# A recurrence and its output stage in one block: half-batches first, POOL and ACT written out

## What is computed

```python
x = x + ttt_linear(layer_norm(group_norm(x)))      # tokens in order, 64 chunks of 16
x = x + relu(W @ [g, descriptor(g)] + bias)         # g = group_norm(x)
```

## Time and profile before

| | us |
|---|---|
| median of 3 runs | 687.34 (686.9 to 690.31) |
| profiled execution | 686.33 |
| its span, first to last instruction | 684.4 |
| PE busy | 523.5 (76%) |
| DVE busy | 492.6 (72%) |
| ACT busy | 332.1 (49%) |
| POOL busy | 376.9 (55%) |

### The profile page before, as it was taken

The page is one execution under the profiler, slowest core; times in us unless marked ns, Lnnn a source line. Parts: engine busy times, 40 slices in busy tenths (PEclk is TensorE's granted clock), DMA queues, the critical chain, the costliest instruction groups (busy, mean ns, idle before and its releaser), DMA issues. The chain is left out here.

```text
span 684.4 us, 30685 instructions
## 1 busy us (share of the span) xinstructions
PE 523.5 (76%) x12150; PEld 364.9 (53%) x12150; DVE 492.6 (72%) x1548; ACT 332.1 (49%) x1044; POOL 376.9 (55%) x659
## 2 busy tenths in 40 slices
PE   0399999996488777777777777777777399859997
PEld 0143344434377666666666666666666155435552
DVE  6356767665678989899999989898998357528331
ACT  0434442225255555555555555555555577544432
POOL 0368888775356555566665556655565647321323
PEclk9999999997555555555555555555555699979999
DMA  9101111114800000000000000000000700000113
GB/s 346 45 12 39 41 31 32 31 31 95 185 4 1 0 0 0 0 0 0 0 0 0 0 0 0 0 0 0 0 2 4 273 5 0 1 1 1 62 69 117
DMA packets 9850, 24.55 MB, mean 36 GB/s; under 512 B 1845, under 2 KB 2510, under 8 KB 9550
## 3 DMA queue, kind: packets, MB, share of 16 engines
q1 hardware_dynamic: 9806, 24.01, 11.4%
HBM read 11.42 MB, written 4.19 MB: 23 GB/s over the span
## 5 line engine op out<-in xcount | busy, mean ns | idle before, releaser
L762 PE MATMUL PS<-work 32*32 32x32 f32 x4064 | 85.5, 238 | 73.1 <-DVE work L911 65.4
L762 PEld LDWEIGHTS PS<-work 32*32 32x32 f32 x4064 | 81.2, 152 | 83.5 <-issue 79.5
L963 POOL TENSOR_TENSOR work<-work,mask 128x256 f32<-128x256 f32 x64 | 46.7, 730 | 83.4 <-DVE work L911 71.8
L751 PE MATMUL PS<-work 64*32 64x64 f32 x2048 | 69.5, 308 | 19.9 <-ACT work L1006 16.9
L500 PE MATMUL PS<-X,work 128*128 (+3 forms) x160 | 72.1, 597 | 6.7 <-ACT X L640 6.4
L751 PEld LDWEIGHTS PS<-work 64*32 64x32 f32 x2048 | 55.3, 162 | 27.2 <-issue 25.9
L774 PE MATMUL PS<-work 32*64 32x32 f32 x2016 | 68.4, 292 | 1.1 <-issue 1.1
L1031 ACT ACTIVATE work<-PS,small 128x128 f32<-128x128 f32 x64 | 23.5, 367 | 80.9 <-PE PS L751 80.9
L774 PEld LDWEIGHTS PS<-work 32*64 32x64 f32 x2016 | 59.7, 216 | 5.3 <-issue 1.3
L500 PEld LDWEIGHTS PS<-X,work 128*128 128x128 f32 (+1 forms) x160 | 25.9, 169 | 47.7 <-issue 47.2
L975 POOL TENSOR_TENSOR work<-work,lrh 128x4 f32<-128x4 f32 x64 | 12.9, 202 | 65.5 <-DVE work L888 62.8
(11 more groups left out here) (146 smaller groups left out, 1314.3 us busy)
## 6 DMA issues: line engine op xcount, KB each, us to landing
X<-in_x SPq DMA_DIRECT2D x4, 1024.0 KB, 8.3
KN<-KP SPq DMA_DIRECT2D x64, 64.0 KB, 1.9
X<-QP SPq DMA_DIRECT2D x8, 512.0 KB, 9.4
KN<-in_x SPq DMA_DIRECT2D x4, 1024.0 KB, 8.8
out<-TT SPq DMA_DIRECT2D x16, 256.0 KB, 2.2
work<-in_rope SPq DMA_DIRECT2D x2, 512.0 KB, 9.8
cst<-in_consts SPq DMA_DIRECT2D x1, 289.0 KB, 5.2
work<-in_wk SPq DMA_DIRECT2D x1, 256.0 KB, 11.4
```

The costliest lines, as they stand in the source:

```text
L751: mm = nc.tensor.matmul(PS[HD * a:HD * a + HD, ZB[p], b * ZW:b * ZW + ZW], KT2[p][r:r + 64, k * B + b, :, :].rearrange("p e t -> p (e t)") ...
L762: mm = nc.tensor.matmul(PS[HD * a:HD * a + HD, bank, b * width:b * width + HD], AM[p][HD * a:HD * a + HD, b, part, :, :].rearrange("p e t ...
L963: nc.gpsimd.tensor_tensor(AM[p].rearrange("p b s e t -> p (b s) e t"), S1[p].unsqueeze(2).broadcast_to([P, 2 * B, E, CS]), mask2.rearrange ...
```

## The change

The second block of the two is folded into the first. The 8 blocks of the output stage are taken in the order ORDER: the first halves of the four batch elements (tokens 0 to 511, chunks 0 to 31), then the second halves. The eight gains of the first four blocks are made on ACT in chunks 40 to 47 (GAIN_AT = 40), one in each; the two sums of the first block on POOL in chunk 56 (PRE_AT = 56). POOL and ACT go over the 64 chunks in plain Python loops, that is, written out with constants; PE keeps `run_chunks`. The loops of the output stage are written out on all engines. The first steps of the output stage are placed between the last outputs of the recurrence on every engine, and no engine waits for the others between the stages. SP loads wsm right behind the permutation, x into KN once the last transposition from KN is done (`tkh`), and the second layer's weights after the last query product. `pre`, `residual`, `statistics`, `output`, `project` (before: `body` on PE) and `follow` (before: `body` on ACT) are as before but for ORDER and constants in the waits. The core of the diff:

```diff
-        def layer_norm(..., ready=None, sums=None):
+        def layer_norm(..., ready=None, sums=None, at=None):
...
-                return src[:, j, ds(i * BLK, BLK)]
+                return src[:, j, ds((i if at is None else at[i]) * BLK, BLK)]
...
+        sq, sd = carve(J, BLK), carve(P)
...
+        ORDER = [i * PER + h for h in range(PER) for i in range(B)]
...
+        q2, ot, act_a, pe_mean, dve_center, act_square, pe_var, act_sd, dve_invert, pe_widen, \
+            dve_scale, act_affine, _, _ = \
+            layer_norm("ln2", TT, sq, sd, eps6, "post_w", "post_b", gain,
+                       4, ready=s_pre, at=ORDER)
...
+            GAIN_AT, PRE_AT = NC // 2 + 8, NC - 8
...
                 run_chunks(pe, body)
+                pe_mean(pe, 0, True)
                 pe.wait_ge(q["gl"], NC)
                 pe.wait_ge(q["am"], NC)
                 grads(HD, QB[1], 1, 0).then_inc(q["attn"], 1)
...
+                pe.wait_ge(s_wo, 16)
+                pe.wait_ge(q["bcopy"], NC)
+                pe_mean(pe, 1, False)
+                pe_var(pe, 0, True)
+                pe_widen(pe, 0, True)
+                for i in range(NBLK):
+                    project(i, i == 0)
...
                 for c in range(NC):
                     body(c, c % 2)
+                dve_center(dve, 0)
                 dve.wait_ge(q["ot"], NC - 4)
                 out_turn(NC - 4)
                 out_r(NC - 3)
...
                 out_r(NC - 1)
+                dve_invert(dve, 0)
+                dve_center(dve, 1)
                 dve.wait_ge(q["ot"], NC - 2)
                 out_turn(NC - 2)
+                dve_scale(dve, 0)
                 dve.wait_ge(q["ot"], NC - 1)
                 out_turn(NC - 1)
...
                     if past(c, 3):
                         out_norm(c - 3, 1 - p)
+                    if c == PRE_AT:
+                        pre(0)
                     pool.wait_ge(q["gl"], c + 1)
...
-                run_chunks(pool, body)
+                for c in range(NC):
+                    body(c, c % 2)
                 for c in (NC - 3, NC - 2, NC - 1):
                     pool.wait_ge(q["rq"], c - NC + 4)
                     out_norm(c, c % 2)
+                    if c == NC - 3:
+                        pre(1)
+                pre(2)
+                pre(3)
...
                         state_b(p)
+                    if GAIN_AT <= c < GAIN_AT + B * J:
+                        i, j = divmod(c - GAIN_AT, J)
+                        act.wait_ge(q["ot"], NC // PER)
+                        gain(act, i, j).then_inc(q2["in"], 1)
                     if not is_last(c):
                         products(c + 1, 1 - p)
...
-                run_chunks(act, body)
-                out_store(NC - 4)
-                out_sd(NC - 2)
-                out_square(NC - 1, 1)
-                out_store(NC - 3)
-                out_sd(NC - 1)
-                out_store(NC - 2)
-                out_store(NC - 1)
+                for c in range(NC):
+                    body(c, c % 2)
...
-                for i in range(4):
-                    act_a(act, i)
                 act_square(act, 0, True)
+                out_store(NC - 4)
+                out_sd(NC - 2)
+                out_square(NC - 1, 1)
+                out_store(NC - 3)
+                out_sd(NC - 1)
                 act_sd(act, 0, True)
+                out_store(NC - 2)
                 act_square(act, 1, False)
                 act_affine(act, 0)
+                out_store(NC - 1)
+                act.wait_ge(q["ot"], NC)
...
+                sp.dma_start(wsm[:, :, :], wo).then_inc(s_wo, 16)
+                sp.wait_ge(s_qperm, 16 * 2 * J * E)
+                sp.wait_ge(q["tkh"], NC)
+                for b in range(B):
+                    sp.dma_start(KN[:, :, b * N:(b + 1) * N], xv[:, :, b, :]).then_inc(s_xr[b], 16)
+                sp.wait_ge(q["qbase"], NC)
+                sp.dma_start(wxt, wx).then_inc(s_w2, 16)
+                sp.dma_start(wsw[0:S, :], ws).then_inc(s_w2, 16)
```

More of the change, by code:

```diff
@@ L699, in build, with gain @@
         ZW = HD + 2 * CS
+        sq, sd = carve(J, BLK), carve(P)
+        spare = KP[:, :, :].rearrange("p j n -> p (j n)")[:, 3 * J * (H + 2 * PAD) * W_:]
+        wxt = spare[:, 0:J * C].rearrange("p (j c) -> p j c", j=J)
+        wsw = spare[:, J * C:J * C + C]
+        s_w2 = sem("w2")
+        s_pre, s_wo, s_o, s_oc, s_x1, s_st2 = (sem(n) for n in ("pre", "wo", "o", "oc", "x1", "stats2"))
+        ORDER = [i * PER + h for h in range(PER) for i in range(B)]
+        s_xr = [sem(f"xr{b}") for b in range(B)]
+        def gain(act, i, j):
+            return nc.scalar.activation(blk_of(TT[:, j, :], ORDER[i]), blk_of(TT[:, j, :], ORDER[i]), ACT.Identity,
+                                        scale=pcol("g", j), bias=pcol("bb", j))
+        q2, ot, act_a, pe_mean, dve_center, act_square, pe_var, act_sd, dve_invert, pe_widen, \
+            dve_scale, act_affine, _, _ = \
+            layer_norm("ln2", TT, sq, sd, eps6, "post_w", "post_b", gain,
+                       4, ready=s_pre, at=ORDER)
         with nc.Block() as block:
@@ L824, in _, with project @@
                 grads(HD, QB[1], 1, 0).then_inc(q["attn"], 1)
+                def project(i, first):
+                    if has(i, 2):
+                        pe_mean(pe, i + 2, False)
+                    if has(i, 1):
+                        pe_var(pe, i + 1, False)
+                    pe.wait_ge(q2["xn"], i * J + J)
+                    for m in range(J):
+                        if m == 1 and has(i, 1):
+                            pe_widen(pe, i + 1, False)
+                        if not first:
+                            pe.wait_ge(s_oc, (i - 1) * J + m + 1)
+                        for j in range(J):
+                            mm = nc.tensor.matmul(PS[:, 2 + m, :], wsm[:, j, m * P:(m + 1) * P], ot(i, j),
+                                                  start=(j == 0), stop=(j == J - 1))
+                        mm.then_inc(s_o, 1)
+                pe.wait_ge(s_wo, 16)
[5 more added lines that the diff above has]
+                    project(i, i == 0)
             @block.vector
@@ L930, in _, with statistics @@
                 out_r(NC - 1)
+                dve_invert(dve, 0)
+                dve_center(dve, 1)
                 dve.wait_ge(q["ot"], NC - 2)
                 out_turn(NC - 2)
+                dve_scale(dve, 0)
                 dve.wait_ge(q["ot"], NC - 1)
                 out_turn(NC - 1)
+                def statistics(i):
+                    for m in range(J):
+                        dve.wait_ge(s_x1, i * J + m + 1)
+                        nc.vector.bn_stats(
+                            stat.rearrange("p (k s) -> p k s", s=6)[:, ORDER[i] * J + m, :],
+                            blk_of(KN[:, m, :], ORDER[i])).then_inc(s_st2, 1)
+                dve_center(dve, 2)
+                dve_invert(dve, 1)
+                dve_scale(dve, 1)
+                for i in range(1, NBLK - 2):
+                    dve_center(dve, i + 2)
+                    dve_invert(dve, i + 1)
+                    statistics(i - 1)
+                    dve_scale(dve, i + 1)
+                dve_invert(dve, NBLK - 1)
+                dve_scale(dve, NBLK - 1)
+                for i in range(NBLK - 3, NBLK):
+                    statistics(i)
             @block.gpsimd
@@ L998, in _ @@
                     out_norm(c, c % 2)
+                    if c == NC - 3:
+                        pre(1)
+                pre(2)
+                pre(3)
+                for i in range(NBLK - 4):
+                    pre(i + 4)
+                    residual(i)
+                for i in range(NBLK - 4, NBLK):
+                    residual(i)
             @block.scalar
@@ L1222, in output, with follow @@
                         act.wait_ge(s_o, i * J + m + 1)
-                        nc.scalar.activation(blk_of(X[:, m, :], i), PS[:, 2 + m, :], ACT.Copy
+                        nc.scalar.activation(blk_of(X[:, m, :], ORDER[i]), PS[:, 2 + m, :], ACT.Copy
                                              ).then_inc(s_oc, 1)
-                def body(i):
-                    if not isinstance(i, int) or i > 0:
+                def follow(i):
+                    if i > 0:
                         output(i - 1)
```

138 lines of the change are left out of this document (23 added, 115 removed).

## The result

The kernel after takes 677.89 us (median of 4 runs, 676.69 to 679.17) against 688.09 us for the kernel before on the same chip: a ratio of 0.985, with an interval of 0.982 to 0.988, so 1.5% faster. The forecast was 679.5 us, with a range of 674.5 to 685.5. The profiled execution took 676.69 us, with a span of 674.9 us against 684.4.

A forecast was written before the change was run, and what follows sets the result against it. The recurrence was taken as a serial chain on VectorE with POOL on it, the output stage as bound by PE. -10.6 + 2.3 - 0.5 + 1.0 = -7.8 on 686.33 profiled gave 678.5, as median 679.5 us; range 674.5 to 685.5.

The forecast's parts named there:

- POOL and ACT written out: Recurrence, 56 periods of the loop: each falls from 5.55 to 5.36 us, -10.6 us.
- Gains in chunks 40 to 47: Eight gains of 0.72 us on ACT, put where it idles 1.12 us for PE: 0.
- The first two sums in chunk 56: Two POOL sums, 2.46 us together, hold VectorE's two-input operations in chunk 56: +2.3 us.
- The seam: Between recurrence and output stage, barrier included: first projection at 550.0 to 550.7 against 551.18, -0.5 us.
- a stall under the early load: Last chunk and tail, beside the early KN load: one stall with 1.0 us on the path, between 0 and 5.2.
- The rest: Output stage's block order and constant waits: 0; last stage untouched.
- Rival (A): Recurrence: the loop isn't what makes POOL late, periods stay 5.55 us, time 690.1 us; chance 0.12.
- (B): Seam pays as meant: mean 1 at full clock (-2.1), no stall (-1.0), time 676.4 us; chance 0.15.
- (C): Chunk 63 and tail: code loading starves under early KN load; 689 us with two stalls, 694 or slower with three; chance 0.13.

The follow-up runs named there:

- u_pool: Kernel before with only POOL's loop over the 64 chunks written out: 676.82 us, ratio 0.983.
- u_act: Kernel before with only ACT's 64 chunks written out: 688.15 us, ratio 0.998.
- u_pe: Kernel before with only PE's 64 chunks written out: 688.84 us, ratio 1.000.
- a_probe: Kernel after with one unused POOL operation added in each of chunks 46 (addition), 49 (copy) and 52 (memset): 679.83 us, a single run.
- a_khx: Kernel after with the khx product moved from POOL to ACT as two scaled copies: 663.45 us, ratio 0.963.
- a_fix: Kernel after with the seam reordered: first two sums behind chunk 63, attention product before mean 0, recurrence's tail before normalisation on VectorE and ACT: 672.64 us, ratio 0.976.
- a_best: Kernel after with the order of a_fix, khx on ACT, and the KN load waiting for the last output: 655.73 us, ratio 0.953.
- a_pretail: Kernel after with the first two sums moved from chunk 56 to behind chunk 63: 679.93 us, ratio 0.987.
- a_fixkhx: Kernel after with both the seam order of a_fix and khx on ACT: 657.23 us, ratio 0.954.
- a_knlate: Kernel after with the load of x into KN waiting for the last output: 677.34 us, ratio 0.984.
- u_both: Kernel before with POOL's and ACT's loops written out, the two stages left apart with their barrier: 676.23 us, ratio 0.983.

## Why the prediction was right, point by point

**POOL and ACT written out, -10.6.** Right, and with the right cause. Chunks 4 to 60 gave -8.12 with chunk 57's +2.08 in them, so -10.2 without. One period, from chunk 5 to 6, is 6.43 where it was 5.89, which more than accounts for the rest. u_pool, u_act and u_pe put the whole of it on POOL. The mechanism is in two steps. POOL's wait in its loop resolves 0.14 us later than in straight code; and POOL's later operations hold VectorE's two-input operations longer (L870 0.53 instead of 0.39 us, L902 0.37 instead of 0.30). The prediction named L876 and L902 for this; the first of the two that gets longer is L870, held by L942, and the prediction did not look at it. a_probe shows the second step by itself (L950 1.32 and 0.64 us instead of 0.29), and a_khx takes away what khx still cost in straight code: 0.29 us a chunk at the median, 14.4 us in all.

**Gains in chunks 40 to 47, 0.** Right. A gain takes 0.82 us there, and L1127 behind it still waits 0.41 for PE, where it waited 1.12. The periods from chunk 41 on are 5.36; the one of chunk 40 is 5.54, behind one of 5.16, so together they cost nothing.

**The first two sums in chunk 56, +2.3.** Measured +2.08. Both L950 and L952 were held (1.31 and 1.35 us), one by each sum; the prediction left open whether VectorE gets in between the two, and it did, only to be held again.

**The seam, -0.5.** The number is exact, -0.50; its make-up isn't. I had mean 1 at 3.75, which it was. I had mean 2 at the full clock, and it took 3.75, too, 1.9 us more. Against that, mean 0 began 2.88 us after the start of chunk 63, not 3.76, and the chain stayed about 1 us ahead of my sum up to the end of sum 2 (21.5 us after that start, where I had 22.6). Part of the 3.76 was a stop of 0.50 us on issue in the trace before, which the trace after doesn't have. The two errors cancelled; that the term is exact is luck. The +1.0 for a stall under the early load stood beside this term and was not there. With it the forecast for this stretch was +0.5. So the step that was off is the stall: not its existence, but its cover. In the kernel after, mean 0 stands in the queue ahead of the attention product, and for 3.4 us PE has work of only four matmuls; that the next instructions arrive meanwhile is my inference. a_fix takes mean 0 away from there, and the product stops for 3.04 us; a_best takes the load away, and 0.4 us is left. That mean 0 is the cover I infer from the order: the four kernels with the early load and mean 0 in front (after, a_probe, a_pretail, a_khx) make the product in 0.45 to 0.65 us, the two with the early load and no mean in front (a_fix, a_fixkhx) stand 3.04 and 2.87. No run had mean 0 in place with a shorter duration.

**The rest, 0.** The output stage gave -0.85 and what follows -0.65, neither forecast, and the first chunks cost +0.73. The stage's -0.85 appears in a_knlate and a_fixkhx too (52.54 us), and not in u_pool or u_both (53.36 and 53.35), which keep the loops of the stage. So it goes with the stage as it is in the kernel after, its loops written out and its blocks in the new order; which of the two gives it, and at which wait, was not tested. The end and the first chunks stay open; I have no run that isolates them.

**The sum.** -7.8 forecast, -9.6 in the profiled executions. The missed 1.8 are the stall that was covered (1.0) and the two small gains behind the seam (1.5), less the first chunks (0.7). The loop's and the sums' errors (+0.4, -0.2) and chunks 60 to 63 (-0.17) nearly cancel. That the total is off by only 1.8 owes something to these signs. The forecast itself was the likeliest case. Rival (A) is out: POOL's loop was the cause. Of (B) one half came true, no stall on the path, and the other didn't, as mean 1 ran at the low clock. The stall of (C) exists (3.04 us in a_fix) but is hidden in the kernel after. Two of my side sums are off and change nothing: (B) took 2.1 us for a mean at the full clock where the term had 1.9, and (C) would be slower than the kernel before from about 12 us of stalls on, not 11.

Seen by its parts, nearly all of the change's gain comes from a side effect, POOL's loop written out. The fold paid nothing as it was written (677.89 against 676.23 without it): it costs 2.1 us in chunk 56 and puts the tail of the recurrence behind the first half of a normalisation. In the other order, and with khx on ACT, it pays 4.5 us.

## What to carry to other kernels

Where VectorE is the serial chain, look for two-input operations of VectorE that end a fixed time after a GpSimd operation (0.15 us here for 128x128, 0.02 for the small L902): they are longer in the profile without being slower. (L918 of the kernel after, a reduction with one input, takes 0.27 us beside khx, and L920 right behind it 0.56.) Compare them with the same line in a chunk where GpSimd has nothing beside it (L946 of a_khx: 0.30 and 0.17 us). The cure is to give the GpSimd work to ACT (14.4 us in a_khx), or to start it sooner (0.14 us sooner gave 0.20 a period in u_pool). Before two stages are folded, write out only the loop of the engine that the fold needs straight, and time that alone; it may be the gain. And when one stage's head is mixed into another's tail, try the tail first on every queue. From a_khx to a_fixkhx the seam fell from 27.84 to 21.44 us; 3.56 of that is means 1 and 2 at the full clock, so the order itself gave about 2.8, with PE's stall laid bare.

## What the runs showed that I had not expected

- PE's granted clock rose while PE was mostly idle and was back down when its work came. In the kernel after it is 1.00 from 533 to 536, with PE busy 1.13 of 3.00 us, and mean 2 behind it takes 3.75 us with 0.50 granted; the mean at 547.61, with 1.00 granted, takes 1.88. In a_fixkhx means 1 and 2 took 1.96 and 1.98. Over the kernels of this case one, two or three of the first three means ran wholly or mostly at the low clock, each worth 1.3 to 1.9 us. What decides it I can't say from one profile of each; the spread of their times (a_fixkhx 654.54 to 659.46 us) is of that size.
- A stall on issue under a large load can stay hidden, here most likely because the work in front of it happens to be long. It came out with a reorder that looked free, and stood 3.04 us in a seam that became only 1.17 us shorter.
- POOL answers a release 0.14 us later in its loop than in straight code (0.51 and 0.37 us from the start of the releasing operation). In the loop the wait is against a register's value, outside against a constant; which of the two, the register or the loop, costs the 0.14 was not separated. For ACT and PE written out no gain showed in the time.
